# Feed forward: the down projection eight tiles behind the up projections

## The reference, cut to what matters

```python
def _mx_dequant(t):               # blocks of 32 along the last axis
    scales = jnp.maximum(max_abs / 448.0, 1e-30)
    q = (blocks / scales[..., None]).astype(jnp.float8_e4m3fn).astype(jnp.float32)
    return (q * scales[..., None]).reshape(rows, feat)

def _mx_linear(x2d, w):
    return _mx_dequant(x2d) @ _mx_dequant(w).T

x2d = layernorm(x)                # 1024 tokens x 512
gate = _mx_linear(x2d, gate_w)    # 2048 x 512 weights
up = _mx_linear(x2d, up_w)        # 2048 x 512
h = jax.nn.silu(gate) * up
out = _mx_linear(h, down_w)       # 512 x 2048
x = x + out
```

## Time and profile before

| | us |
|---|---|
| median of three runs | 2136.52 |
| the profiled execution | 2135.23 |
| its span | 2133.4 |
| feed forward, steps 0 to 7, 1789.3 to 1883.5 | 94.2 |
| its middle, 1883.5 to 2103.8 | 220.3 |
| its end, 2103.8 to 2124.6 | 20.8 |

### The profile page before, as it was taken

One profiled execution on the slowest core, in us unless ns is written; L12 is line 12 of the kernel. 1 busy time (PEld: TensorE's weight loads), 2 busy tenths in 40 slices (PEclk: granted clock), 3 DMA queues, 4 the chain that ended last, 5 costly groups with the idle time before them and its releaser, 6 DMA issues. The chain is left out here.

```text
span 2133.4 us, 24875 instructions
## 1 busy us (share of the span) xinstructions
PE 1935.3 (91%) x9621; PEld 1409.3 (66%) x9624; DVE 1168.6 (55%) x2069; ACT 635.2 (30%) x1013; POOL 219.6 (10%) x185
## 2 busy tenths in 40 slices
PE   7899795899997599979999999999899998899996
PEld 6677783444433458847886886877758744688885
DVE  5412737555543345547674684665643378656653
ACT  3311322444444055514340331322224221222110
POOL 0000001111201100000120120210200001112221
PEclk9999896899998599999999999999999999999998
DMA  5100402222210500014221313203202100110101
GB/s 198 40 1 0 158 11 67 67 68 58 64 37 1 158 0 1 1 36 140 77 79 66 114 54 116 97 20 117 80 31 70 60 20 22 58 37 25 39 1 40
DMA packets 67125, 124.12 MB, mean 58 GB/s; under 512 B 8512, under 2 KB 26944, under 8 KB 65472
## 3 DMA queue, kind: packets, MB, share of 16 engines
q1 hardware_dynamic: 67008, 122.53, 18.1%
HBM read 88.82 MB, written 14.68 MB: 49 GB/s over the span
## 5 line engine op out<-in xcount | busy, mean ns | idle before, releaser
L941 DVE TENSOR_REDUCE b_nm<-ps 128x1 f32<-128x1024 f32 x128 | 151.5, 1220 | 118.8 <-PE ps L862 118.8
L929 ACT ACTIVATE b_pr<-ps 128x512 f32<-128x512 f32 x256 | 132.3, 605 | 159.5 <-PE ps L880 159.5
L229 PE MATMUL ps<-d_x_high,d_w_high 128*128 128x512 f32 x384 | 154.8, 403 | 4.4 <-DVE d_w_low L1767 4.4
L230 PE MATMUL ps<-d_x_low,d_w_high 128*128 128x512 f32 x384 | 150.4, 392 | 0.0
L231 PE MATMUL ps<-d_x_high,d_w_low 128*128 128x512 f32 x384 | 150.3, 392 | 0.0
L892 PE MATMUL ps<-b_pr,b_VS 128*64 128x512 f32 x512 | 130.6, 634 | 0.0
L1544 PE MATMUL ps<-d_wo,d_ga 128*128 128x512 f32 x256 | 110.6, 593 | 1.5 <-DVE d_ga L1745 1.5
L880 PE MATMUL ps<-b_qS,b_kS 98*128 98x512 f32 x256 | 92.3, 442 | 20.1 <-DMA b_qS<-b_nm_parts 17.7
L862 PE MATMUL ps<-b_kS,b_qS 96*128 96x512 f32 x256 | 95.0, 461 | 15.6 <-DMA b_qS<-b_q_parts 10.1
L880 PEld LDWEIGHTS ps<-b_qS,b_kS 98*128 98x128 f32 x256 | 44.1, 192 | 90.7 <-issue 52.1
L1659 POOL TENSOR_TENSOR d_sqsum<-d_sqsum,d_sq 128x512 f32<-128x512 f32 x32 | 42.4, 1325 | 487.4 <-ACT d_sq L1604 487.2
(11 more groups left out here) (372 smaller groups left out, 4592.5 us busy)
## 6 DMA issues: line engine op xcount, KB each, us to landing
b_kS<-b_k_parts SPq DMA_DIRECT2D x96, 128.0 KB, 2.3
f_rows<-d_fw SPq DMA_DIRECT2D x24, 512.0 KB, 3.0
f_w<-f_rows SPq DMA_DIRECT2D x12, 1024.0 KB, 4.8
b_qS<-b_q_parts SPq DMA_DIRECT2D x96, 64.0 KB, 2.0
a_convT<-in_convT SPq DMA_DIRECT2D x4, 1024.0 KB, 12.8
b_ctxT<-in_ctxT SPq DMA_DIRECT2D x8, 512.0 KB, 5.1
d_w<-in_d_wq SPq DMA_DIRECT2D x16, 256.0 KB, 4.4
d_w<-in_d_wk SPq DMA_DIRECT2D x16, 256.0 KB, 4.3
```

Source lines behind the costliest of these rows:

```text
L229: nc.tensor.matmul(out, lhsT[0], rhs[0], start=start, stop=False)
L230: nc.tensor.matmul(out, lhsT[0], rhs[1], start=False, stop=False)
L929: nc.scalar.activation(pr[:, n % RING, :], c.ps[:, 4 + n % BANKS, :], ACT.Exp).then_inc(exp_done, 1)
L941: nc.vector.tensor_reduce(nm[:, g % 2, u:u + 1], c.ps[:, banks:banks + 2, :], AX.XY, ALU.max, negate=True).then_inc(job_read, 1)
```

## The change

`LAG` goes from 3 to 8: the down product of a tile comes a whole chunk behind its up products, so steps 0 to 7 have none, and steps 32 to 39 have nothing else. `HR` stays 8. The weight turns of the first chunk move: none in steps 0 to 4, the four of the first down weights in step 5 behind both products, four of the next gate weights in step 6 and four up weights in step 7. In later chunks they stand in steps 2 to 7 of the chunk, not 0 to 5. `w_places(s)` says which turns stand before the gate product, between the two, and behind them. The units of x are scaled and rounded in steps 0, 2 and 4, one in each. The rounding of a unit of h moves from two steps after its second tile to five, with the scales where they were but for the first three units; the last two are rounded in steps 33 and 34. GpSimd does the ratios of two units first, and then always the products of one unit and the ratios of the unit two later.

```diff
-    STEPS, LAG, HR, XU = NCH * TT, 3, 8, TT // 2
+    STEPS, LAG, HR, XU = NCH * TT, TT, TT, TT // 2
@@ w_turns
         n, t = s // TT, s % TT
-        j = 3 * n + 2 + t // 2
-        return [("w", j, 2 * (t % 2)), ("w", j, 2 * (t % 2) + 1)] if t < 6 and j < len(FJOBS) else []
+        if n == 0:
+            j, count = t - 3, KD
+        else:
+            j, count = 3 * n + 1 + t // 2, 2
+        first = 0 if n == 0 else 2 * (t % 2)
+        return [("w", j, first + i) for i in range(count)] if 3 * n + 2 <= j < len(FJOBS) else []
+
+    def w_places(s):
+
+        fresh = w_turns(s)
+        if s == 5:
+            return [], [], fresh
+        return fresh[:len(fresh) // 2], fresh[len(fresh) // 2:], []
+
+    SCALED_AT = {4: [0], 5: [1], 6: [2]} | {2 * u + 1: [u] for u in range(3, STEPS // 2)}
+    ROUNDED_AT = {2 * u + 6: [u] for u in range(STEPS // 2 - 2)} | {STEPS + 1: [STEPS // 2 - 2], STEPS + 2: [STEPS // 2 - 1]}
@@ GpSimd
+            ratios(XU)
+            ratios(XU + 1)
             for u in range(XU, XU + STEPS // 2):
-                ratios(u)
                 products(u)
+                if u + 2 < XU + STEPS // 2:
+                    ratios(u + 2)
@@ vector engine
-            unit_scales(1)
             for s in range(STEPS + LAG):
                 for r in x_turns(s):
                     low(r)
-                if s + 1 < XU:
-                    unit_round(s + 1)
-                    if s + 2 < XU:
-                        unit_scales(s + 2)
+                if s in (0, 2, 4):
+                    unit_scales(1 + s // 2)
+                    unit_round(1 + s // 2)
                 if s >= LAG:
                     low(("h", s - LAG))
-                fresh = w_turns(s) if s < STEPS else []
-                for r in fresh[:1]:
+                early, middle, late = w_places(s) if s < STEPS else ([], [], [])
+                for r in early:
                     low(r)
-                if s >= 2 and s % 2 == 0 and s <= STEPS:
-                    unit_round(XU + s // 2 - 1)
-                for r in fresh[1:]:
+                for u in ROUNDED_AT.get(s, []):
+                    unit_round(XU + u)
+                for r in middle:
                     low(r)
...
-                    if s % 2 == 1:
-                        unit_scales(XU + s // 2)
+                    for r in late:
+                        low(r)
+                    for u in SCALED_AT.get(s, []):
+                        unit_scales(XU + u)
@@ TensorE
-                    fresh = w_turns(s)
-                    for r in fresh[:1]:
+                    early, middle, late = w_places(s)
+                    for r in early:
                         turn(r)
...
                     up(s, 2 + s % 2, gT, silu_done, g_done)
-                    for r in fresh[1:]:
+                    for r in middle:
                         turn(r)
                     up(s, 4 + s % 2, uT, h_done, u_done)
+                    for r in late:
+                        turn(r)
@@ scalar engine
-                    for r in w_turns(s):
+                    early, middle, late = w_places(s)
+                    for r in early:
                         high(r)
...
                     nc.scalar.activation(silu[:, s % 2, :], c.ps[:, 2 + s % 2, :], ACT.Silu).then_inc(silu_done, 1)
+                    for r in middle + late:
+                        high(r)
```

## The result

The kernel after takes 2126.18 us, the median of seven runs (2120.72 to 2131.65), beside 2136.52 of before (seven runs, 2130.99 to 2140.37). The ratio is 0.9954, with a 95% interval from 0.9937 to 0.9970: faster by a little under half a per cent. The prediction said 2129 us, with 2121 to 2137 as its range.

A forecast was written before the change was run, and what follows sets the result against it. The prediction took TensorE, busy throughout the middle, as the bound, with only beginning and end able to move. Beginning -14.3, middle 0 and end +8.3 sum to -6.0 us from the profiled 2135.23: 2129 us, range 2121 to 2137.

The forecast's parts named there:

- The bound: Last stage: TensorE is busy for all 220.3 us of the middle, so only the beginning and the end can move.
- Beginning: Last stage up to the start of step 8: 63.9 us, a change of -14.3 us with five down products moved out.
- the clock: Time lost to TensorE's slowed clock in the beginning: 3 us, 1 behind wait A and 2 behind wait B.
- wait A: Before step 2, TensorE waits 2.8 us for pair 1 of x and the subtraction after its turn.
- wait B: Eight late turns behind the products of step 5 take 8.15 us, 3.6 of it work, so 4.6 us of waiting.
- Middle: The 220.3 us between beginning and end: a change of 0, with operands ready and the up weights' load hidden.
- End: Eight down products alone behind the last up: +8.3 us, from a bare +3.3 and 5.0 for the meeting with GpSimd.
- The single lone step: In the end, turn, copy, subtraction and product in a row take 4.9 us for each down product standing alone.
- The meeting with GpSimd: Second lone step: GpSimd's two operations delay a rounding, the third step's subtraction comes 2.85 us late, its product runs 2 slower.
- The gain in full: Rival: the third lone step waits only 0.25 us, end +4.1, total -10.2, 2125 us; chance 0.25.
- the stalls are kept: Rival: waits A and B each cost 2.5 us of clock, plus a gate-weight wait in step 6; 2133.5 us; chance 0.15.
- The slow end: Rival: TensorE at 1.2 GHz through all eight lone products, total +10, 2145 us; chance 0.08.

The follow-up runs named there:

- e2_round_early: Changed kernel with the scales and roundings of x and h, and GpSimd's order, as before; late turns kept; 2137.88 us, ratio 1.0013 to before.
- e1_ratio_first: Changed kernel with GpSimd doing the ratios of the last unit of h ahead of the products of unit 13; 2123.64 us, ratio 0.9946 to before.
- e3_turns_early: Changed kernel with the weight turns where they were before, deferred roundings kept; 2136.51 us, ratio 1.0014 to before.
- e5_turn_ahead: Changed kernel with the next h's turn issued ahead of each lone down product, its subtraction ahead of the addition, from step 31; 2119.72 us, one run.
- e7_scales_behind: Changed kernel with the scales of unit 1 of h moved from step 5 to step 6, right ahead of the first rounding of h; 2128.05 us, one run.
- e8_best: Changed kernel with h turns issued ahead, last three roundings in steps 31, 32, 34, unit 1 scales in step 6, first down weights turned in step 3; 2109.93 us, ratio 0.9890.

## Why the prediction was right, point by point

**The bound.** The reading that only the beginning and the end of the stage can move held: the middle has TensorE busy for all of its 219.9 us, and TensorE did not wait there in any variant.

**Beginning, -14.3 against -15.6.** To the start of step 8 63.9 us were forecast and 62.6 measured. The places and the order of the waits were right, and so was the length of each hole to within 0.3 us (2.57 for 2.8, 0.98 for 1.15, eight turns in 8.0 for 8.15). Inside the eight turns the division was not: the idle is 3.58 for 4.6, and the turns themselves take about 1 us more than the 3.6 they were given. The term that was mis-sized is the clock: I took 3 us, 1 behind wait A and 2 behind wait B. Behind A the clock was 0.54 for 3.7 us, which is 3.7 x 0.46 = 1.7 us lost; behind B it was 1.00 and nothing was lost. 1.7 for 3 gives the 1.3 us of difference. That B cost nothing could not have been read off its idles: in `e2_round_early` the same eight turns, with less idle in them, ran into a stretch at 0.50. The two clock terms missed in opposite directions, and that their sum came within 1.3 us is in part luck.

**Middle, 0 against -0.4.** The load of the up weights, the operands and the deferred rounding were hidden, as said.

**End, +8.3 against +8.1.** The single lone step was 4.9 us, as read from the last three steps of before. The meeting with GpSimd came in the step that the order named. From the third lone turn to the fourth it is 2088.72 - 2079.01 = 9.7 us, 4.8 above a bare step: 2.54 of additional idle (4.00 - 1.46) and 2.3 for the slow product, against 2.85 and 2. `e1_ratio_first` shows the cause. The trace agrees in kind with the Trainium skill here (SBUF — State Buffer, section "Who interferes with whom"), which has one of the two engines blocked while the other holds the shared ports: 3.21 us for 0.76 beside two multiplications, 1.49 beside one. GpSimd pays a little too: its second operation, at whose begin the first bit operation was still running, took 2.10 for 1.92.

**The rivals.** The gain in full is out: the third step waited 4.00. That the stalls are kept is out as well: no wait for gate weights in step 6, and a clock loss of 1.7 in all of the beginning. The slow end is out: only one of eight lone products ran slow, the one behind 4.00 us of idle, and the granted clock was 1.00 in each of the five steps behind it, with 1.46 us idle in each 4.9. The rule of the Trainium skill that spoke for it (TensorE: Matmul & The Clock Gate, section "A second HAM failure mode: psum-queue depth-cycling") did not decide here.

**The total.** Of the 10.5 us in the two profiled executions 7.8 are the change's, 1.8 more than predicted, and 2.6 are the spread of where the stage begins. The medians differ by 10.3, with 6.4 to 13.5 as the interval; which share of the 2.5 us between medians and stage is chance these runs do not settle.

What the prediction did not see is how narrow the gain is. It treated the late turns and the deferral as one thing and never priced them apart. `e2_round_early` and `e3_turns_early` show that either alone, with the distance, would have been no gain at all.

## What to carry to other kernels

When a software pipeline is made deeper, its drain is the price. Let each lone step of the drain issue the transposes of the next one ahead of its own product: here that took the 1.46 us of idle out of every lone step, and with three roundings moved it was worth 17.7 us, over twice what the deeper pipeline had won. Whether the kernel before, with its distance of three, would have gained as much from it was not tried. Work that has slack should leave the in-order queue together with everything else that stands before the same consumer; taking one of two obstacles away gained nothing in the sum here. And before a scale or any other producer for GpSimd is moved, look at what the vector engine does right behind it: bit operations there pay for the meeting.

## What was not expected of the hardware

The two bit operations of a rounding (alone 0.75 us) took 1.49 beside one multiplication of GpSimd that was already running, 2.41 beside one that started right after them, and 3.21 beside two in a row. Each of these came again wherever the same meeting did: 3.21 or 3.22 in `e3_turns_early`, `e5_turn_ahead` and `e7_scales_behind`, 2.42 in `e8_best`. The subtraction for a product beside GpSimd shows no such growth (2082.83 in the kernel after, 0.67 beside an operation that began at 2082.39).

The length of an idle alone does not tell whether TensorE's clock falls. Behind idles of 2.27 (`e1_ratio_first`), 2.32 (before) and 1.59 + 0.98 (after) the next product ran near half rate; behind 2.69 and 2.67 in `e3_turns_early` and 2.82 in `e7_scales_behind` it did not:

```profile
1820.40:1825.40 5.00, 4.98 (x26) 4.23 (x27) 2.19 (x4) 1.69 (x3) 0.00 (x0) 1.00 0.09 15
1838.20:1843.20 5.00, 4.96 (x26) 4.20 (x27) 3.73 (x10) 1.68 (x3) 1.92 (x1) 1.00 0.10 16
```

(`e3_turns_early`, the stretches behind its waits of 2.69 and 2.67.) In `e8_best`, behind a wait of 2.81 in the same place of the program as the 2.82, the clock was 0.73 over the next 5.9 us. With the eight turns of `e2_round_early` this makes two places where the same order of instructions ran at both clocks. What differs there was not tried.
